# Reciprocal roots on GpSimd: a power in place of guess and refinement on VectorE, in a fused metaformer block

## The reference

```python
# first part
z    = layernorm(_ln_c(x)) * ln1_w + ln1_b            # two norms, folded into one root
proj = (z @ lrp_w.T + lrp_b) * mask * sigmoid(z @ gate_w.T + gate_b)
left, right = split(proj)                             # 32 channels each
tri  = einsum('bikc,bjkc->bijc', left, right)         # one 128x128x128 product per channel
go   = sigmoid(tri @ og_w.T + og_b)
z2   = layernorm(tri, ln2_w, ln2_b) @ op_w.T          # "the triangle's norm", eps 1e-5
x    = x + tri + go * (z2 + out_bias)                 # called x1 in the kernel
# second part, a mixture of 8 experts, the best 2 of each token
t    = x as tokens
h    = (t - mean) / sqrt(var + 1e-5)                  # "the second token norm"
p    = softmax(h @ router_w + router_b); top_p, top_i = top_k(p, 2); top_p /= sum(top_p)
t    = t + sum over the two experts of top_p * (h @ expert_w[top_i] + expert_b[top_i])
```

## Time and profile before

| | |
|---|---|
| median of 3 runs | 191.41 us (190.51 to 192.46) |
| the profiled execution | 191.88 us, of which the span of its instructions is 190.1 us |
| busy share of the span | TensorE 76%, VectorE 81%, ScalarE 42%, POOL 48% |
| chain of work that ended last | TensorE 43%, VectorE 37%, ScalarE 6%, POOL 5%, issue 5%, DMA 2% |
| granted TensorE clock | 0.862 over the span; 1.00 from 63 to 103 us, 0.95 from 103 to 111, 0.61 from 111 to 126.7, 0.68 from 126.7 to 136, 0.91 from 136 to 190 |
| VectorE busy | 9.97 of the 15.7 us from 63 to 78.7; 22.4 of 24.3 to 103; 7.5 of 8 to 111; 14.7 of 15.7 to 126.7 |

### The profile page before, as it was taken

The page is one execution under the profiler, slowest core; times in us unless marked ns, Lnnn a source line. Parts: engine busy times, 40 slices in busy tenths (PEclk is TensorE's granted clock), DMA queues, the critical chain, the costliest instruction groups (busy, mean ns, idle before and its releaser), DMA issues.

```text
span 190.1 us, 2813 instructions
## 1 busy us (share of the span) xinstructions
PE 144.0 (76%) x905; PEld 95.6 (50%) x906; DVE 153.4 (81%) x266; ACT 79.6 (42%) x149; POOL 90.4 (48%) x75
## 2 busy tenths in 40 slices
PE   6577808398779799958999368280898598999982
PEld 2236506176569699957999357220443224323321
DVE  0889799968478159999899998999499988799951
ACT  3337542145612486224666634222335246433322
POOL 1230994437840694235435164467527622555520
PEclk9885795559999999999999956667569979999998
DMA  5995000000000000000000000668970783788112
GB/s 142 360 442 238 0 0 0 2 0 0 3 0 0 3 2 0 3 0 0 0 3 0 2 0 0 152 157 206 207 166 0 180 206 81 159 197 287 55 57 110
DMA packets 5533, 16.26 MB, mean 86 GB/s; under 512 B 1296, under 2 KB 1296, under 8 KB 5392
## 3 DMA queue, kind: packets, MB, share of 16 engines
q1 hardware_dynamic: 5520, 16.11, 30.2%
HBM read 5.62 MB, written 2.10 MB: 41 GB/s over the span
## 4 chain that ended last, share of the span: by engine, by line
PE 43%; DVE 37%; ACT 6%; POOL 5%; issue 5%; DMA 2%; POOLq 0%; DVEq 0%; ACTq 0%
PE ps L852 9%; PE ps L839 7%; PE ps L725 4%; POOL gates L356 4%; PE ps L690 3%; DVE stats L1091 3%; DVE xk L1125 3%; DVE lr L1007 2%; PE ps L772 2%; PE ps L789 2%; DVE stats L976 2%; PE ps L743 2%; DMA xk<-in_x_k 2%; DVE triF L1237 2%; PE ps L675 2%
## 5 line engine op out<-in xcount | busy, mean ns | idle before, releaser
L356 POOL TENSOR_TENSOR gates<-gates,late_sb 128x512 f32<-128x512 f32 x16 | 20.6, 1298 | 14.4 <-ACT gates L493 14.4
L839 PE MATMUL ps<-w3F,selb 96*128 96x512 bf16 (+1 forms) x64 | 22.1, 413 | 4.4 <-DVE triF L1237 2.4
L690 PE MATMUL ps<-w1m,ring 64*128 64x256 f32 x128 | 22.1, 501 | 1.5 <-ACT ring L470 1.5
L394 POOL TENSOR_TENSOR sq<-sq,cb 128x512 f32<-128x512 f32 x8 | 12.8, 1598 | 19.3 <-DVE sq L1113 19.3
L690 PEld LDWEIGHTS ps<-w1m,ring 64*128 64x128 f32 x128 | 15.6, 248 | 5.9 <-issue 1.5
L839 PEld LDWEIGHTS ps<-w3F,selb 96*128 96x128 bf16 x64 | 5.4, 102 | 23.8 <-DVE triF L1237 8.3
L1007 DVE TENSOR_TENSOR lr<-ps,gates 128x512 f32<-128x512 f32 x16 | 10.9, 689 | 7.1 <-POOL gates L356 7.0
L1091 DVE TENSOR_REDUCE stats<-gates 128x16 f32<-128x512 f32 x16 | 10.9, 680 | 5.4 <-ACT gates L527 5.2
L675 PE MATMUL ps<-early_sb,ring 128*128 128x128 f32 x32 | 6.8, 351 | 10.7 <-DVE lr L1007 9.1
L408 POOL TENSOR_TENSOR lr<-lr,stats 128x512 f32<-128x512 f32 x8 | 10.9, 1380 | 7.2 <-DVE stats L1153 7.2
L385 POOL TENSOR_TENSOR xi<-xi,tri (+1 forms) x8 | 9.9, 1276 | 9.1 <-DVE tri L1084 9.1
(11 more groups left out here) (125 smaller groups left out, 352.7 us busy)
## 6 DMA issues: line engine op xcount, KB each, us to landing
xi<-ring SPq DMA_DIRECT2D x32, 128.0 KB, 2.4
xk<-ring SPq DMA_DIRECT2D x32, 128.0 KB, 2.3
xi<-in_x_i SPq DMA_DIRECT2D x1, 2048.0 KB, 13.1
out<-lr SPq DMA_DIRECT2D x8, 256.0 KB, 2.1
xk<-in_x_k SPq DMA_DIRECT2D x4, 256.0 KB, 5.6
xk<-in_x_k SPq DMA_DIRECT2D x2, 512.0 KB, 7.0
late_sb<-in_late SPq DMA_DIRECT2D x1, 874.5 KB, 8.7
early_sb<-in_early SPq DMA_DIRECT2D x1, 513.0 KB, 5.2
```

Source lines behind the costliest of these rows:

```text
L356: pool.tensor_tensor(v, v, m, ALU.mult).then_inc(s_gm, 1)
L394: pool.tensor_tensor(v, v, cb[:, :].unsqueeze(1).broadcast_to([P, JG, C]), ALU.add)\
L690: m = pe.matmul(ps[:, 4 * slot + 2 * p + b, q % 2 * 2 * F1:(q % 2 + 1) * 2 * F1], fring[rows, slot * W + q * P:slot * W + (q + 1) * P], w1 ...
L839: pe.matmul(ps[:, SPREAD[n % 4], :], selb[0:KW, n * P:(n + 1) * P], w3F[0:KW, bass.ds(g * W, W)], start=True, stop=True).then_inc(s_wb, 1)
```

## The change

On VectorE the variance step makes the whole variance (1/C and eps instead of halves of them) and signals; guess and all refinements of the triangle's norm and of the second token norm are gone, and with them their waits. On POOL a new function `root(n, variance, done)` waits for the variance of half n and writes `rstd` of 128 x 64 as one `tensor_tensor` with the operation `pow`, its exponent -0.5 broadcast from a column that is set at the start. It stands in POOL's program at four places: after the fifth residual, after the eighth residual (ahead of the first `shifted`), ahead of the first `xhat`, and between `xhat(2)` and `rank(0, 2)`. VectorE's `update` now waits for the root of its half. The first token norm keeps its roots.

```diff
--- before.py
+++ after.py
@@ -97,6 +97,7 @@
         nmean, ssum, std, rstd = (stats[:, n * N:(n + 1) * N] for n in range(4))
         ones_b = sb("ones_b", P, BF16)
         warm = sb("warm", W, BF16)
+        power = sb("power", 1)
         lnb = sb("lnb", P)
         lnb2 = sb("lnb2", P)
         w1in = sb("w1in", R * F1)
@@ -192,6 +193,9 @@
         s_o = sem("result_T_ready")
         s_out = sem("out_stored")
         s_rstd = sem("rstd_ready")
+        s_tvar = sem("tri_variance_ready")
+        s_trstd = sem("tri_rstd_ready")
+        s_xvar = sem("x1_variance_ready")
         s_pick2 = [sem(f"second_picked{n}") for n in range(2)]
         s_w2 = [sem(f"second_weighed{n}") for n in range(2)]
 
@@ -339,6 +343,7 @@
         def _(pool):
             pool.memset(ones_b[:, :], 1.0).then_inc(s_ones, 1)
             pool.memset(warm[:, :], 1.0).then_inc(s_ones, 1)
+            pool.memset(power[:, :], -0.5).then_inc(s_ones, 1)
 
 
             def centred(n):
@@ -384,7 +389,20 @@
             def residual(g, slot):
                 pool.tensor_tensor(xi[:, bass.ds(g * W, W)], xi[:, bass.ds(g * W, W)],
                                    tri[:, bass.ds(g * W, W)], ALU.add).then_inc(s_res, 1)
-            groups(pool, residual)
+            for g in range(5):
+                residual(g, g % 2)
+
+            def root(n, variance, done):
+
+                pool.wait_ge(s_ones, 3)
+                pool.wait_ge(variance, n + 1)
+                at = slice(n * HN, (n + 1) * HN)
+                pool.tensor_tensor(rstd[:, at], ssum[:, at], power[:, 0:1].broadcast_to([P, HN]), ALU.pow)\
+                    .then_inc(done, 1)
+            root(0, s_tvar, s_trstd)
+            for g in range(5, G):
+                residual(g, g % 2)
+            root(1, s_tvar, s_trstd)
 
 
             def shifted(g, slot):
@@ -418,11 +436,13 @@
                                    .broadcast_to([P, HN, E]), ALU.mult).then_inc(s_w2[n], 1)
 
 
+            root(0, s_xvar, s_rstd)
             pool.wait_ge(s_rstd, 1)
             xhat(0)
             xhat(1)
             rank(0, 0)
             xhat(2)
+            root(1, s_xvar, s_rstd)
             rank(0, 2)
             xhat(3)
             second_weighed(0)
@@ -989,11 +1009,8 @@
 
             def tri_variance(n):
 
-                link(dve.tensor_scalar(half_of(ssum, n), half_of(ssum, n), 0.5 / C, 0.5 * LN_EPS, ALU.mult, ALU.add))
-                guess(half_of(rstd, n), half_of(ssum, n))
-
-            def refine_half(n):
-                refine(half_of(rstd, n), half_of(ssum, n), half_of(std, n))
+                dve.tensor_scalar(half_of(ssum, n), half_of(ssum, n), 1.0 / C, LN_EPS, ALU.mult, ALU.add)\
+                   .then_inc(s_tvar, 1)
 
             def scaled(g, slot):
 
@@ -1099,8 +1116,6 @@
             tri_variance(0)
             for g in range(G // 2, G):
                 sums(s_q4, s_v4, 0)(g, g % 2)
-                if g - G // 2 < ITERATIONS:
-                    refine_half(0)
             dve.wait_ge(s_v4, G)
             tri_variance(1)
 
@@ -1108,6 +1123,7 @@
             def update(g, slot):
 
                 dve.wait_ge(s_go, g + 1)
+                dve.wait_ge(s_trstd, g * 2 // G + 1)
 
                 wait(dve, s_x1, g - 1)
                 dve.tensor_tensor(grid(sq[:, slot * W:(slot + 1) * W]),
@@ -1132,30 +1148,8 @@
             def half_variance(n):
 
                 dve.wait_ge(s_v5, (n + 1) * G // 2)
-                mark(n, dve.tensor_scalar(half_of(ssum, n), half_of(ssum, n), 0.5 / C, 0.5 * LN_EPS,
-                                          ALU.mult, ALU.add))
-
-            def half_guess(n):
-                after(n)
-                mark(n, dve.tensor_scalar(half_of(rstd, n).bitcast(I32), half_of(ssum, n).bitcast(I32), -0.5,
-                                          float(GUESS), ALU.mult, ALU.add))
-
-            def refine_a(n):
-                after(n)
-                mark(n, dve.tensor_tensor(half_of(std, n), half_of(rstd, n), half_of(rstd, n), ALU.mult))
-
-            def refine_b(n):
-                after(n)
-                mark(n, dve.tensor_tensor(half_of(std, n), half_of(std, n), half_of(ssum, n), ALU.mult))
-
-            def refine_c(n, final=False):
-                after(n)
-                m = dve.scalar_tensor_tensor(out=half_of(rstd, n), in0=half_of(std, n), scalar=-1.5,
-                                             in1=half_of(rstd, n), op0=ALU.add, op1=ALU.mult)
-                if final:
-                    m.then_inc(s_rstd, 1)
-                else:
-                    mark(n, m)
+                dve.tensor_scalar(half_of(ssum, n), half_of(ssum, n), 1.0 / C, LN_EPS, ALU.mult, ALU.add)\
+                   .then_inc(s_xvar, 1)
 
             def of(tile, n, inner=E):
                 return tile[:, n * HN * inner:(n + 1) * HN * inner]
@@ -1250,23 +1244,11 @@
                 if t > 0:
                     close(t - 1, (t - 1) % 2)
 
-                if t < ITERATIONS:
-                    refine_half(1)
                 if X1_LAG + 1 < t < G:
                     sums5(t - X1_LAG - 2)
                 if t == G - 1:
                     half_variance(0)
-                    half_guess(0)
-                    refine_a(0)
-                    refine_b(0)
-                    refine_c(0)
-                    refine_a(0)
-                    refine_b(0)
-            refine_c(0)
-            refine_a(0)
             sums5(G - 4)
-            refine_b(0)
-            refine_c(0, final=True)
 
             scale_logits(0)
             sums5(G - 3)
@@ -1281,18 +1263,10 @@
             largest(rest, gap, 0)
             half_variance(1)
             candidates(rest, gap, second, 0)
-            half_guess(1)
             difference(0)
-            for k in range(ITERATIONS):
-                refine_a(1)
-                if k == 0:
-                    top_rank(second, 0, 2)
-                if k == 1:
-                    pick_second(0)
-                refine_b(1)
-                if k == 2:
-                    weigh_first(0)
-                refine_c(1, final=(k == ITERATIONS - 1))
+            top_rank(second, 0, 2)
+            pick_second(0)
+            weigh_first(0)
 
             add_second(0)
             scale_logits(1)
```

## The result

The changed kernel took 224.56 us (median of 4 runs, 223.99 to 225.35) against 191.94 us for the kernel before (190.51 to 192.57): a ratio of 1.17, 95% interval 1.163 to 1.180. I had forecast 188.5 us in a range that ended at 196.2.

The account below looks back on a forecast made before the run. It took the chain as TensorE's from 87.77 to 103.02 us, then mostly VectorE's to 134, with shared SBUF ports setting the rest. Stage 1 -2.4 and stage 2 -0.5 made -2.9: 188.5 us, range 186.2 to 196.2.

Parts of the forecast that it names:

- The length of one power: One 128x64 power on POOL, shown by no row: taken as 1.5 us, with ends 0.29 and 3.4.
- the formula on record: Change in total time: 2p-5.9 us up to p=1.5, then -2.9 + 4(p-1.5); nil at 2.2.
- p: The time of one power of 128x64 on POOL, taken as 1.5 us; forecast case 0.8 to 1.75.
- its steps depend on each other: Rival: the power's steps are dependent and not overlapped, p 2.7 or more; 196.1 us at 3.4, 202.5 at 5; chance 0.32.
- three places: Where a dear power hurts: second triangle power before the first shift, root before group 7's sum, that before the second ranking.
- Stage 1: Triangle's norm: roots on POOL bring x1 of group 1 2.4 us earlier at p=1.5; each us above costs two.
- Stage 2, the ports: Second token norm, first half: the power holds the shared ports, delaying group 7's sum; second variance step earlier by 1.95-p.
- the ports aren't held: Rival: a power leaves VectorE's two-input steps free, -4.6 us in all, 186.8 us; chance 0.10.
- Stage 2, the second ranking: Second token norm, second half: the power stands ahead of the second ranking and delays the logit difference; gain 1.55-p.
- Transfers, residuals and the memset: No transfer bounds an earlier start, nobody needs a residual before the first x1, and the extra small memset costs nothing.
- The gain hoped for: At p=1.5, -2.4 us in stage 1 and -0.5 in stage 2, in all -2.9.

Follow-up runs that it names:

- the plain product: Changed kernel with its four powers replaced by plain products of the same 128x64 operands on POOL: 185.36 us, ratio 0.954 to the kernel before.
- k = 16: Changed kernel with each root a power on 16 of its 64 columns, a plain product on the rest: 193.8 us, ratio 1.016 to the kernel before.
- k = 8: Changed kernel with each root a power on 8 of its 64 columns, a plain product on the rest: 188.38 us, ratio 0.988 to the kernel before.
- token norm only: Kernel before with POOL powers only in the second token norm, the triangle's norm kept on VectorE: 208.0 us, ratio 1.078.
- ScalarE's: The same roots made by a square root on ScalarE and a reciprocal on VectorE, no power: 185.91 us, ratio 0.967 to the kernel before.
- the spare power: Kernel before plus one unused 128x64 power on spare tiles behind POOL's fifth residual: 192.53 us in one execution, against 192.58.

## Why the prediction was wrong, step by step

- **The length of one power: wrong, and the cause of the miss.** The step was that at a plain pass's price "a dozen steps make 0.18 + 12 x 0.108 = 1.5, and thirty make 3.4". It assumed that each step of a software routine costs what a plain POOL pass costs per column. Measured: 10.55 us for 128x64, 0.159 us per column. The rows of before held nothing to size the routine by, and I drew the upper end from the same assumption as the middle. A bound that shares its assumption with the estimate is no bound. With the measured 10.7 the formula on record gives -2.9 + 4 x 9.2 = +33.9, 225.3 us; measured was 224.56. That it comes so close is partly luck: the stages have +32.05, with 2.2 and 0.55 less than the formula in stage 2 and about 1 more in stage 1. The prediction's two signs of being wrong both came up: p outside 0.8 to 1.75, and VectorE running two-input steps during a power.
- **What the trace can't show about a library routine** stood in the rival I gave 0.32, "its steps depend on each other", which had 202.5 us for a power of 5 us. Its sign was right, and so were two of its three places; the root did not hold up group 7's sum. Its price was too low. Whether the routine is a chain of dependent steps no run here shows; only its length is shown. The Trainium skill, GPSIMD Engine Reference, section 7, gives 4 cycles per element for each step of such a chain; with its 1.2 GHz the 0.159 us per column would be some 48 of them, an estimate.
- **Stage 1: right, to 1 us.** The stage is -2.4 up to p = 1.5 and -2.4 + 2(p-1.5) above. Measured were -2.29 with the plain product, -1.53 (formula -1.6) at 1.9, +1.92 (+0.9) at 3.15 and +16.65 (+15.7) at 10.55. The 1 us on top in the last two goes with TensorE's clock. The chain of waits of the changed kernel, a pair of gate matmuls just after the long wait and the same pair 1.5 us later:

```profile
101.58 0.53 PE ps L792 x2
...
103.06 0.28 PE ps L792 x2
```

  The first pair takes 0.53 and the second 0.28: 1.2 GHz and 2.4 GHz. The stretch as a whole (busy us of each engine, then the granted clock, 0.67):

```profile
78.00:104.00 26.00, 9.21 (x52) 8.70 (x52) 7.19 (x9) 2.41 (x5) 21.11 (x8) 0.67 0.00 0
```

  TensorE had waited for x1 until then; in the kernel before the clock was at 1.00 from 63 to 103 us. With k = 16 it was 0.50 from 85.6 to 89.0, again on the gate matmuls after the wait, and with k = 8 and the plain product it was 1.00 throughout. So the longer wait goes with the fall, and the fall costs about 1 us. That the wait alone brings it about is not shown: "token norm only", without a longer wait there, had 0.50 from 86.3 to 89.7 and lost 0.66.
- **Stage 2, the ports: wrong.** The step on group 7's sum, that it "comes after the power was queued, and ends at 107.87+p", failed: the sum takes 0.69 during the power (122.86 above). So up to the second variance step the change gains 2.2 us until the power is longer than the VectorE work beside it, and costs p-4.2 beyond. The rival "the ports aren't held", chance 0.10, was right in this, though it forecast a faster kernel (186.8). The Trainium skill, SBUF — State Buffer, "Who interferes with whom", calls the port pair that VectorE and GpSimd share an exclusive lock, and says that a VectorE instruction with two SBUF inputs contends with a GpSimd instruction that reads SBUF. The rows of plain products and sums here agree (a shift of 1.64 holds back a sum to 1.57), the powers do not: with two inputs from SBUF they let 128x64 and 128x512 steps with two SBUF inputs through at 0.22 and 0.69.
- **Stage 2, the second ranking: right in kind, 0.55 too dear.** p-1.55 on record, p-2.1 measured at four lengths, where the logit difference, which the prediction let wait, runs during the power (142.25 above).
- **Transfers, residuals and the memset: nothing to see, as said.** The tail moved by -0.3 to +1.0 us in all kernels of the change, whatever p was.
- **The gain hoped for is real:** -2.3, -2.2 and -1.5 by stages with a plain product of 0.3 to 0.6 us in the root's place, and -2.3, -1.5 and -1.5 with ScalarE's.

## What to carry to other kernels

Before a chain of cheap steps on a busy engine is replaced by one instruction on an idle one, measure that instruction by itself at its size; if that can't be done and no row shows a similar routine, let the range follow from how often it stands on the path (here four times), not from a guess at its inside. Count where it queues on its new engine: the second power of the triangle cost the most not for the updates that need it but for the shifts behind it (no run here put the shifts ahead of it). And where an engine's table switches fit into its waits, two instructions on two engines can deliver a root sooner than ten steps on one.

## What the runs showed of the hardware

- A GpSimd `tensor_tensor` power costs 0.159 us per column plus 0.36 (10.55 us for 128x64), the same on 1 and on 128 partitions, and, for 128x64, the same for exponents -0.5, 0, 0.5, 1 and 2.
- It does not keep VectorE from reading two SBUF inputs while it runs: such steps took 0.22 (128x64) and 0.69 us (128x512) in it, as they do alone. Started while one of them was in flight, it took 10.85 in place of 10.55, as the plain product took 0.60 in place of 0.29.
- VectorE's small steps met a power with less loss than they met plain residuals: beside the spare power the variance step and the guess took 0.20 us each instead of 0.87 and 1.19, and the first update came 13.9 us after the first residual instead of 15.25.
